# Group 0 with its x rows stationary and W1 streaming, its x turned by TensorE, its bias spread by DRAM

## The reference

```
hidden = concat([cond, cond], -1)                      # [4, 512]
fused  = concat([x, mean(x, axis=1), hidden], -1)      # mean and hidden repeated over the 1024 rows
out    = x + relu(fused @ W + b)
```

## Time and profile before

| | us |
|---|---|
| median of 3 runs | 103.4 (103.25 to 103.8) |
| the profiled execution | 103.63 |
| its span | 101.7 |
| PE busy | 97.2 |
| DVE busy | 83.0 |
| ACT busy | 47.1 |
| POOL busy | 38.9 |

### The profile page before, as it was taken

One profiled execution on the slowest core, in us unless ns is written; L12 is line 12 of the kernel. 1 busy time (PEld: TensorE's weight loads), 2 busy tenths in 40 slices (PEclk: granted clock), 3 DMA queues, 4 the chain that ended last, 5 costly groups with the idle time before them and its releaser, 6 DMA issues.

```text
span 101.7 us, 1713 instructions
## 1 busy us (share of the span) xinstructions
PE 97.2 (96%) x523; PEld 78.5 (77%) x523; DVE 83.0 (82%) x148; ACT 47.1 (46%) x116; POOL 38.9 (38%) x35
## 2 busy tenths in 40 slices
PE   5989999999999999999999999999999999999980
PEld 2348999988888786888888886888888886888870
DVE  3172789899899899999999984999999993996670
ACT  3285435895418279496397001874744003710000
POOL 1029800000000002999848500568578059950000
PEclk9999999999999999999999999999999999999999
DMA  1999999999999998999999388000591690299994
GB/s 38 269 303 290 273 268 282 273 251 266 318 256 231 269 251 221 246 234 226 345 331 286 106 195 219 0 0 0 113 267 32 134 259 20 67 283 273 248 325 144
DMA packets 35438, 21.39 MB, mean 210 GB/s; under 512 B 2020, under 2 KB 33128, under 8 KB 35432
## 3 DMA queue, kind: packets, MB, share of 16 engines
q1 hardware_dynamic: 33848, 20.13, 77.4%
q10 hardware_dynamic: 1584, 1.18, 3.9%
HBM read 12.91 MB, written 8.39 MB: 209 GB/s over the span
## 4 chain that ended last, share of the span: by engine, by line
PE 90%; DMA 4%; ACT 1%; DVE 1%; ACTq 0%; issue 0%
PE ps_y L472 77%; PE ps_y L573 4%; PE ps_y L575 4%; PE ps_y L574 4%; DMA xa<-in_x_dram 4%; PE ps_mean L491 1%; PE ps_const L540 1%; ACT xh L267 1%; DVE ps_xt L341 1%; ACT w1h L260 1%; DVE w L462 0%; ACTq L160 0%; PE ps_y L596 0%
## 5 line engine op out<-in xcount | busy, mean ns | idle before, releaser
L240 POOL TENSOR_TENSOR xa<-xa,back 128x512 f32 (+1 forms) x26 | 33.5, 1318 | 44.7 <-DVE back L354 44.7
L472 PE MATMUL ps_y<-xh,w1h 128*128 (+2 forms) x128 | 43.6, 368 | 0.4 <-ACT w1h L260 0.3
L472 PE MATMUL ps_y<-xl,w1h 128*128 (+2 forms) x128 | 43.0, 363 | 0.0
L472 PE MATMUL ps_y<-xh,w1l 128*128 (+2 forms) x128 | 42.8, 363 | 0.0
L267 ACT ACTIVATE xh<-ps_xt 128x512 fp32r<-128x512 f32 (+1 forms) x36 | 19.7, 549 | 17.4 <-DVE ps_xt L341 17.4
L472 PEld LDWEIGHTS ps_y<-xh,w1h 128*128 128x128 f32 x128 | 22.6, 189 | 5.4 <-issue 1.1
L347 DVE TENSOR_TENSOR xl<-ps_xt,xh 128x512 fp32r<-128x512 f32 (+1 forms) x36 | 22.1, 617 | 4.9 <-ACT xh L267 4.9
L472 PEld LDWEIGHTS ps_y<-xh,w1l 128*128 128x128 f32 x128 | 22.6, 189 | 3.8
L472 PEld LDWEIGHTS ps_y<-xl,w1h 128*128 128x128 f32 x128 | 22.7, 189 | 3.6
L341 DVE STREAM_TRANSPOSE ps_xt<-xa 128x512 f32<-128x512 f32 (+1 forms) x36 | 22.3, 642 | 3.6 <-DMA xa<-in_x_dram 3.3
L285 ACT ACTIVATE relu_t<-ps_y,bias 128x512 f32<-128x512 f32 x20 | 13.5, 686 | 16.8 <-DVE bias L388 15.3
(11 more groups left out here) (35 smaller groups left out, 37.1 us busy)
## 6 DMA issues: line engine op xcount, KB each, us to landing
xa<-in_x_dram SPq DMA_DIRECT2D x60, 128.0 KB, 3.8
out_dram<-xa SPq DMA_DIRECT2D x28, 256.0 KB, 4.1
w<-in_L_cond_W_dram SPq DMA_DIRECT2D x4, 256.0 KB, 5.5
w<-in_L_cond_W_dram SPq DMA_DIRECT2D x2, 512.0 KB, 6.7
w<-in_x_dram SPq DMA_DIRECT2D x4, 256.0 KB, 4.6
out_dram<-w SPq DMA_DIRECT2D x3, 256.0 KB, 3.4
xa<-in_x_dram ACTq DMA_DIRECT2D x4, 128.0 KB, 4.4
w<-in_L_cond_W_dram SPq DMA_DIRECT2D x4, 64.0 KB, 3.4
```

Of the source, the lines that this page charges most:

```text
L240: nc.gpsimd.tensor_tensor(rows, rows, back[:, t], ALU.add).then_inc(added, 1)
L472: return nc.tensor.matmul(ps_y[:, t, ls], lhs, rhs, start=start, stop=stop, skip_group_check=True)
```

## The change

Group 0 is computed as the last group is: 128 rows of x stationary, 512 columns of W1 streaming, results in rows.

- x of group 0 is loaded in rows, into `x0`, in four blocks of 128 rows (r); the first two are split between SP and ACT by partitions. The W1 quarters of slices 2 and 3 are all issued by SP.
- VectorE puts each block's columns in W1's order (`order_x0`, into `w3`, which is free then; SP waits for the turns before it loads w3). TensorE turns 128x128 blocks by a product with a unit matrix (`turn_x0`), made by POOL, into `ps_xt` (the very first into `ps_const`). ScalarE makes the high part of a whole block of 128 x 512 (`x0_high`), VectorE the low part (`x0_low`) and, as the high part's accumulator is no longer used, the sums (`x0_sum`).
- W1's slice 0 is cast half by ScalarE, half by VectorE.
- TensorE: WARM is 5 instead of 14, three short ones (256 columns) come after the first turns, then 48 products of 512 columns in an order written out over blocks and slices.
- Results are saved into `w1`'s space in rows. The bias of batch 0 goes by DRAM onto all partitions (`first_bias`; issued by ScalarE around its first four relus), POOL adds it after its first four residuals, VectorE does relu and x (`add_first`, two at group 3 and two at group 5), SP stores after group 4.
- SAVED is 4 (group 1 alone), lists run over groups 1 to 6, and TensorE's loop is written out.

```diff
-WARM = 14
+WARM = 5
+WARM_2 = 3
...
+        def x0_part(r, all_k=False):
+            return 1 if r == 0 and not all_k else r + 2
+        def turned_x0(r, ks=slice(0, NK)):
+            bank = ps_const[:] if r == 0 and ks.stop == 1 else ps_xt[:, r % XT_BANKS]
+            return bank.rearrange("p (k l) -> p k l", k=NK)[:, ks]
...
# sync
-            load_x0(sp, 0, LOW)
+            load_x0(sp, 0, 0, P // 2)
             load_w1(sp, 0, 1, LOW)
+            load_x0(sp, 1, 0, P // 2)
             load_w1(sp, 1, 2, LOW)
-            load_w1(sp, 2, NK, LOW)
-            load_x0(sp, 1, LOW)
+            load_x0(sp, 2)
+            load_w1(sp, 2, NK, ORDER)
+            load_x0(sp, 3)
...
             load_x(sp, 3, ORDER)
+            sp.wait_ge(x0t_ready, NR + 1)
...
+                if g == SLOTS:
+                    for r in range(NR):
+                        sp.wait_ge(first_added, r + 1)
+                        sp.dma_start(out_rows[0, :, r], x0[:, r]).then_inc(stored, 16)
...
# gpsimd
+            nc.gpsimd.memset(unit[:], 1.0).then_inc(unit_filled, 1)
+            pool.wait_ge(unit_filled, 1)
+            nc.gpsimd.affine_select(out=unit[:], in_=unit[:], pattern=[[-1, P]], compare_op=ALU.is_equal, fill=0.0,
+                                    base=0, channel_multiplier=1).then_inc(unit_ready, 1)
...
+            for t in range(NK):
+                residual(0, t, t + 1)
+            pool.wait_ge(first_bias_landed, 16)
+            for r in range(NR):
+                pool.wait_ge(y_saved, r + 1)
+                nc.gpsimd.tensor_tensor(y0[:, r], y0[:, r], first_bias[:], ALU.add).then_inc(first_biased, 1)
...
# scalar
-            load_x0(act, 0, HIGH)
+            load_x0(act, 0, P // 2, P)
             act.wait_ge(ones_set, 1)
             nc.scalar.activation(act_warm[:], ones[:, 0:1], ACT.Relu)
             load_w1(act, 0, 1, HIGH)
+            load_x0(act, 1, P // 2, P)
             load_w1(act, 1, 2, HIGH)
-            load_w1(act, 2, NK, HIGH)
-            load_x0(act, 1, HIGH)
...
+            x0_high(0, slice(0, 1))
             w1_high(0)
+            x0_high(0, slice(1, NK))
+            x0_high(1)
             w1_high(1)
+            x0_high(2)
+            w1_high(2)
+            w1_high(3)
+            x0_high(3)
+            n_x = pieces_to(1)
+            x_high(n_x)
+            x_high(n_x + 1)
+            save_rows(0)
+            x_high(n_x + 2)
+            save_rows(1)
+            x_high(n_x + 3)
+            save_rows(2)
+            save_rows(3)
...
+            act.wait_ge(bias_summed, 1)
+            act.dma_start(first_line.rearrange("(j e) -> j e", j=NQ), bias_row[0:P:Q, 0]).then_inc(first_stored, 16)
             for n in range(len(tiles)):
                 relu(n)
+                if n == SAVED - 1:
+                    act.wait_ge(first_stored, 16)
+                    act.dma_start(first_bias[:], first_line.partition_broadcast(P)).then_inc(first_bias_landed, 16)
...
# vector
+            def order_x0(r, ks=slice(0, NK)):
+                if ks.start == 0:
+                    dve.wait_ge(x0_landed[r], 16 * 2 if r < 2 else 16)
+                nc.vector.tensor_copy(x0_blocks[:, r].rearrange("p (k j m) -> p k j m", k=NK, j=NQ)[:, ks],
+                                      by_block(x0[:, r])[:, ks]).then_inc(x0_ordered, 1)
...
+            order_x0(0, slice(0, 1))
+            order_x0(0, slice(1, NK))
+            x0_low(0, slice(0, 1))
+            dve.wait_ge(w1_landed[0], 16 * NQ)
+            nc.vector.tensor_copy(as_tiles(w1h[:, 0])[:, DVE_T:NK], by_tile(w1[:, 0])[:, DVE_T:NK]).then_inc(w1h_rest_ready, 1)
+            order_x0(1)
+            x0_low(0, slice(1, NK))
+            x0_sum(0, slice(0, 1))
+            x0_sum(0, slice(1, NK))
+            x0_low(1)
+            order_x0(2)
+            x0_sum(1)
+            x0_low(2)
+            order_x0(3)
+            x0_sum(2)
+            x0_low(3)
+            x0_sum(3)
...
+            def add_first(r):
+                dve.wait_ge(first_biased, r + 1)
+                nc.vector.scalar_tensor_tensor(out=x0[:, r], in0=y0[:, r], scalar=0.0, in1=x0[:, r],
+                                               op0=ALU.max, op1=ALU.add).then_inc(first_added, 1)
...
# tensor
+            def turn_x0(r):
+                if r == 0:
+                    pe.wait_ge(unit_ready, 1)
+                if r >= XT_BANKS:
+                    pe.wait_ge(x0l_ready, x0_part(r - XT_BANKS, True))
+                    pe.wait_ge(x0_summed, x0_part(r - XT_BANKS, True))
+                for k in range(NK):
+                    if k < 2:
+                        pe.wait_ge(x0_ordered, x0_part(r, k > 0))
+                    last = nc.tensor.transpose(turned_x0(r, slice(k, k + 1))[:, 0], x0_blocks[:, r, P * k:P * k + P], unit[:])
+                    if k == NK - 1 or r + k == 0:
+                        last.then_inc(x0t_ready, 1)
...
+            turn_x0(0)
+            for _n in range(WARM_2):
+                nc.tensor.matmul(ps_mean[:, 0:HL], warm[:, 0:P], warm[:, 0:HL], start=True, stop=True)
+            rows_high(0, 0)
+            rows_low_x(0, 0)
+            turn_x0(1)
+            rows_low_w(0, 0)
+            rows_high(1, 0)
+            rows_low_w(1, 0)
+            rows_low_x(1, 0)
+            rows_high(0, 1)
+            rows_low_x(0, 1)
+            rows_high(1, 1)
+            rows_low_x(1, 1)
+            turn_x0(2)
+            rows_low_w(0, 1)
+            rows_low_w(1, 1)
+            for k in (0, 1):
+                rows_high(2, k)
+                rows_low_x(2, k)
+                rows_low_w(2, k)
+            for k in (2, 3):
+                for r in range(3):
+                    rows_high(r, k)
+                    rows_low_x(r, k)
+                if k == 2:
+                    turn_x0(3)
+                for r in range(3):
+                    rows_low_w(r, k)
+            for k in range(NK):
+                rows_high(3, k)
+                rows_low_x(3, k)
+                rows_low_w(3, k)
```

More of the change, by code:

```diff
@@ L50, in build, with steps_of_x @@
     assert B == 4 and NK % XT_BANKS == 0 and NK == Y_BANKS == BACK_RING and RELU_RING == H * NK
-    pieces = [(0, l, HL, k) for l in (0, HL) for k in range(NK)]
-    pieces += [(g, 0, NL, k) for g in range(1, G) for k in range(NK)]
+    pieces = [(g, k) for g in range(1, G) for k in range(NK)]
     def pieces_to(g):
-        return NK * g + NK * (g > 0 if isinstance(g, int) else 1)
-    tiles = [(g, t) for g in range(LAST) for t in range(NK)]
+        return NK * (g - 1)
+    tiles = [(g, t) for g in range(1, LAST) for t in range(NK)]
     DVE_ADDS = 2
-    SAVED = H * NK
-    def steps_of_x(n, ahead):
-        return 1 if SLOTS <= n // NK + ahead < G else 0
+    SAVED = NK
+    def steps_of_x(g, ahead):
+        return 1 if SLOTS <= g + ahead < G else 0
+    DVE_T = NK // 2
     xv = x.rearrange("b (h lb lm) (j e) -> (b h) j lm lb e", h=H, lm=Q, j=NQ)
@@ L134, in build @@
         ps_mean = psum("ps_mean", [P, NL])
-        x0_landed = [sem(f"x0_landed{h}") for h in range(2)]
+        x0_landed = [sem(f"x0_landed{r}") for r in range(NR)]
         x_landed = [sem(f"x_landed{g}") for g in range(G)]
@@ L155, in build, with load_x0 @@
         last_hi_ready, last_hl_ready = sem("last_hi_ready"), sem("last_hl_ready")
-        def load_x0(eng, half, quadrants):
-            lbs = slice(half * LB // 2, (half + 1) * LB // 2)
-            for j in quadrants:
-                eng.dma_start(xa[Q * j:Q * j + Q, 0, lbs], xv[0, j, :, lbs]).then_inc(x0_landed[half], 16)
+        def load_x0(eng, r, first=0, end=P):
+            eng.dma_start(x0[first:end, r], x_rows[0, first:end, r]).then_inc(x0_landed[r], 16)
         def load_x(eng, g, quadrants):
@@ L207, in _ @@
                 sp.dma_start(last_x[:, r], x_rows[LAST, :, r]).then_inc(last_x_landed, 16)
-            for g in range(LAST):
+            for g in range(1, LAST):
                 if g == LAST - 2:
@@ L312, in _ @@
             x_high(n_x + 1)
-            save(NK + 3)
+            save(3)
             x_high(n_x + 2)
@@ L384, in sum_bias @@
                 dve.wait_ge(mean_done, b + 1)
-                nc.vector.scalar_tensor_tensor(out=bias_row[:], in0=ps_mean[:, 0:P], scalar=1.0 / L, in1=const_row[:],
+                nc.vector.scalar_tensor_tensor(out=bias_row[:, b], in0=ps_mean[:, 0:P], scalar=1.0 / L, in1=const_row[:],
                                                op0=ALU.mult, op1=ALU.add).then_inc(bias_summed, 1)
                 dve.wait_ge(bias_summed, b + 1)
-                nc.vector.transpose(bias[:, b], bias_row[:].rearrange("p (t b) -> p t b", b=Q)).then_inc(bias_ready, 1)
+                nc.vector.transpose(bias[:, b], bias_row[:, b].rearrange("p (t b) -> p t b", b=Q)).then_inc(bias_ready, 1)
             def turn_and_split(first, end):
                 for n in range(first, end):
-                    early = n + 1 < end and pieces[n + 1][3] > 0
+                    early = n + 1 < end and pieces[n + 1][1] > 0
```

(22 more changed lines are left out.)

207 lines of the change are left out of this document (97 added, 110 removed).

## The result

| | before | changed |
|---|---|---|
| median of 4 runs each, same chip | 103.60 (103.25 to 103.93) | 109.82 (108.39 to 110.85) |
| profiled execution | 103.63 | 108.39 |
| its span | 101.72 | 106.44 |

The changed kernel is slower by 5.3% (ratio 1.0529, 95% from 1.0466 to 1.0591). The prediction had the sign but not the size: 104.0, with an upper end of 104.9. The ratio leaves out the two slowest runs of the changed kernel (110.07 and 110.85, over 1.5% above its fastest) as being in a slower state, so it is smaller than the quotient of the two medians.

The account below looks back on a forecast made before the run. It took TensorE's chain of waits as the bound: a start of 7.06 us, TensorE work, a short tail. Group 1's start +0.1 and hole +0.45, rounded +0.6, gave 104.2 profiled, 104.0 median; range 103.5 to 104.5, over all 102.4 to 104.9.

Parts of the forecast that it names:

- the hole: In group 1, TensorE waits 0.45 us for VectorE's low parts; bounds none to 0.9.
- First product: 5.3: Group 0's first product on TensorE starts at 5.3, which is 1.75 us earlier than 7.06.
- I take 4.7: W1's slice 0, second and third issue of each DMA queue, lands at 4.7 us.
- Turns at 0.09: Each 128x128 turn on TensorE takes 0.09 us; twelve cost 1.05 (0.7 to 3.0), or 3.3 by the skill page.
- Idle about 0.9 ... about 0.7: TensorE idles in group 0 ahead of the low parts of blocks 1 and 2, 1.6 us together.
- 19.1: Predicted start of group 1 on TensorE, against 18.98 before: +0.1, the early start spent on idle time and turns.
- Rival 3: TensorE's clock rises near 9 instead of 6 after fewer warm-ups: +0.9, 104.9 us; chance 0.19.
- products run from 5.3: Argument against a late clock rise: TensorE has products to run from 5.3 us.
- Rival 2: Reduction and casts are short enough for group 1, so no hole: +0.1, 103.5 us; chance 0.21.
- rival 1: Row blocks reach TensorE in time and the early start is kept: -0.8, 102.6 us; chance 0.28.
- +0.5 against 3.4 us of slack: VectorE drops four turns back (2.6) and gains four adds (3.1); its slack takes the +0.5, costed at nothing.
- The time moves by how far the first product of group 1 moves, plus any hole: Products of groups 1 to 7 stay the same, so only group 1's start (+0.1) and the hole (+0.45) count.

Follow-up runs that it names:

- run 15: The changed kernel measured once more, unchanged, in more rounds: median 108.88 us, ratio 1.0474 to the kernel before.
- run 13: run 1 with block 1's ordering copy reading block 0's x, so block 1's products are not with its own x: 107.34 us, ratio 1.0375.
- run 1: The changed kernel with 7 warm-ups instead of 5 and 5 short ones instead of 3: 107.92 us, ratio 1.0416.
- run 14: run 1 with POOL starting W1's first low part only once block 1's ordering copy is done: 107.53 us, ratio 1.0393.
- run 12: The changed kernel with the edits of run 1 and run 3 and a later bias load, adds left on VectorE: 106.51 us, ratio 1.0239.
- 5: The changed kernel with group 0's relu on ScalarE, its x adds on POOL and its stores one group earlier: 111.01 us, ratio 1.0738.
- run 2: The kernel before with 5 warm-ups instead of 14, nothing else: 105.44 us, ratio 1.0175.
- run 3: The changed kernel with the turns of row blocks 2 and 3 moved earlier in TensorE's list: 107.82 us, ratio 1.0419.
- runs 9 and 10: The kernel before plus one unused VectorE add pair, ahead of group 5's turn back (9: ratio 1.0065) or of batch 2's bias (10: 0.9977).

## Why the prediction was wrong in size

On the profiled execution it said 104.2; measured 108.39. The 4.2 between them are 3.1 at group 1's start, 0.1 at the hole and 0.9 at the end.

**"First product: 5.3": failed, 6.47.** "I take 4.7" for W1's slice 0 rested on the landing rows of the two first DMAs. ScalarE's second and third issues took 1.21 us (1.52 to 2.73) where 0.46 each had been carried over, and the slice landed at 5.93 (at 5.0 to 5.5 in the other profiles, with the same issues). The +1.17 did not all reach group 1: with the first product at 5.90, 0.57 earlier, group 1 started at 22.23 all the same (run 15), as block 1's turns came no earlier. The other profiles with the new start have it at 5.7 to 6.3.

**"Turns at 0.09": 0.11 at the full level, 0.22 at the lower** (0.45 and 0.87 for four in the chain). Twelve at 0.11 would be +0.3. By TensorE's page of the Trainium skill (TensorE: Matmul & The Clock Gate, Part 4: PE-mode transpose) a transpose in a kernel takes about 275 ns (its figures are for bf16, these turns are f32). As the duration of one turn the trace agrees: the four from 11.63 start 0.11 apart and end after 0.60, so the last lasts 0.27. But turns overlap, and the next product starts 0.36 after the first (11.99). The estimate of 3.3 for twelve took a duration for a distance.

**"Idle about 0.9 ... about 0.7", 1.6 in all: 3.4, with the slow products in it.** From 6.47 to 22.21 are 15.74, of which 48 x 0.229 and 12 x 0.11 are 12.3. The waits stood where the prediction put them, ahead of blocks 1 and 2, but longer. With the clock up and block 1 out of the way (run 13: 5.96 to 20.71) 2.4 remain. What the runs took out of group 1's start: the clock 0.7 (run 1), then the copy behind POOL up to 0.56 (run 14), or block 1's landing and copy together 0.8 (run 13), or, by turning blocks 2 and 3 earlier, up to 0.9 (run 12 against 1), which the order of the changed kernel's TensorE list gives away. These overlap and don't add up. Of the 3.1, run 1 and run 13 together take 1.5; by the terms of the sum, the remaining 1.6 against 19.1 are a first product near 5.96 (0.66), turns (0.3), and 0.8 more idle than the 1.6, less 0.2 by which my 19.1 was above the sum of its parts. Block 2's landing and copy are in that 0.8 with other short waits; how it divides is not shown.

**The copy beside POOL was not in the sum at all.** Three DVE forms grew beside POOL: the copy (0.43 to between 1.02 and 1.52), the first mean term (0.49 to 1.48) and the operations with two SBUF inputs (three mean terms 2.33 to 3.24 and 5.04, the add pair 1.29 to 2.13). Subtractions from PSUM stood at 0.67 beside it. The Trainium skill (SBUF — State Buffer, Who interferes with whom) has the rule: VectorE and GpSimd share one pair of ports, which the operation that starts first holds to its end, and a two-port copy or an operation with two SBUF inputs blocks on it. By it the copy asked for at 6.44 would start when POOL's row ends, 7.22, and end near 7.65. It ended at 7.49, so the trace agrees to 0.16. In each of the eight profiles in which POOL's first subtraction was under way when block 1's copy began, the copy ended 0.27 to 0.29 after it.

**Rival 3, the late rise, was real and rated too low.** Given 0.19 and +0.9 for a rise near 9. It rose at 8 to 13 in every profile with 5 and 3 warm-ups. Against run 1 it cost 0.7 at group 1 with the rise at 10.9 and 1.85 with the rise at 13.3 (5); in the kernel before, the cut costs 2.3 there. Of the two arguments, "products run from 5.3" was the weak one: products ran from 7.06 in run 2 and the rise still took until 12.9. The rule that the prediction cites there (transposes don't count) is not needed for that: run 2 has no turns. No run tests it.

**The hole: right.** 0.45 said, 0.57 measured, where the prediction put it, and gone once VectorE gets its blocks sooner (run 3). Rival 2, no hole, and rival 1, the feed keeps up, are refuted.

**"+0.5 against 3.4 us of slack": failed.** The adds were even shorter than taken (0.65 each, not 0.78); what failed is the slack. The 3.4 was TensorE's busy time less VectorE's over a window, and the comparable window of the changed kernel still shows two us of it:

```profile
43.79:88.49 44.70, 44.70 (x210) 36.20 (x209) 42.49 (x69) 20.09 (x48) 26.52 (x21) 1.00 0.63 153
```

But idle time can be used only where it lies. VectorE's is in the waits for the mean: 1.67 ahead of batch 2's bias, 0.66 ahead of batch 3's, and the second comes after D5. The first pair just fitted into the first (0.19 left). Mean terms grown by 1.9 beside POOL found room ahead of it only because VectorE began them at 60.06 instead of 57.91, 2.15 later where all around them was 3.8 later. The second pair stood where there was no wait.

**"The time moves by how far the first product of group 1 moves, plus any hole": incomplete.** It took the chain of waits for the only path. The stores are a second one, 14 us long and without slack, that hangs on VectorE at D5; runs 9 and 10 separate it. +0.9 in the profile; the late pair alone costs the kernel before 0.7 to 0.8 us.

## What to carry to other kernels

Put an engine's added work against the waits in its own timeline between two due dates, never against the busy share of a window; and where the last stores run without a break, treat their first issue as an end of its own and ask which engine feeds it. Warm-ups may only be cut after a run of the old kernel with the cut alone. A copy or a two-input operation in SBUF that is moved onto VectorE has to be priced beside whatever POOL does at that moment.
